# Loading W's second chunk in the last attention group, and a new order of the first two tiles' work

## The reference, cut to what matters

```
x = x + xattn(layernorm(x), ctx, ctx)          # x, ctx: (8, 512, 2048)
    per head and channel: corr = ifft(fft(q) * conj(fft(k))) over 512 positions
    w, idx = top_k(corr, 12);  w = softmax(w)
    out[p] = sum_i w_i * v[min(idx_i + p, 511)]
n = layernorm(x)
x = x + n @ W + bias + (n @ A_b) @ B_b + (n @ A_s) @ B_s   # W: 2048 x 2048
    A_b, B_b: rank 32, summed over 16 adapters by the batch's gate
```

## Time and profile before

| | |
|---|---|
| median of 3 runs | 3106.81 us (3106.17 to 3109.11) |
| the profiled execution's own time | 3107.9 us |
| its span, first to last instruction | 3106.1 us |
| PE busy | 3018.6 us, 97% |
| DVE, POOL, ACT busy | 2077.8, 1659.4, 1120.5 us |
| mean granted TensorE clock | 0.990 of full speed |

### The profile page before, as it was taken

One profiled execution on the slowest core, in us unless ns is written; L12 is line 12 of the kernel. 1 busy time (PEld: TensorE's weight loads), 2 busy tenths in 40 slices (PEclk: granted clock), 3 DMA queues, 4 the chain that ended last, 5 costly groups with the idle time before them and its releaser, 6 DMA issues. The chain is left out here.

```text
span 3106.1 us, 37964 instructions
## 1 busy us (share of the span) xinstructions
PE 3018.6 (97%) x14387; PEld 1647.6 (53%) x14387; DVE 2077.8 (67%) x2742; ACT 1120.5 (36%) x1696; POOL 1659.4 (53%) x753
## 2 busy tenths in 40 slices
PE   5999999999999999999977999999999999999999
PEld 3566565665656566665643444444444444444444
DVE  6889898989989999999994445444444443344322
ACT  4666666666656666555521011110111111011100
POOL 4898898988979898988842122221221122112210
PEclk9999999999999999999998999999999999999999
DMA  6334434344444534334159444345344534434321
GB/s 229 134 125 150 153 135 170 119 156 146 136 162 146 173 135 165 126 129 160 64 191 267 155 132 125 117 136 150 105 130 125 145 105 134 153 109 136 95 79 41
DMA packets 281220, 430.27 MB, mean 139 GB/s; under 512 B 147489, under 2 KB 164001, under 8 KB 265633
## 3 DMA queue, kind: packets, MB, share of 16 engines
q1 hardware_dynamic: 145888, 394.43, 36.7%
q10 hardware_dynamic: 135168, 33.57, 6.0%
HBM read 308.15 MB, written 86.25 MB: 127 GB/s over the span
## 5 line engine op out<-in xcount | busy, mean ns | idle before, releaser
L1439 PE MATMUL ps<-w_hi,h_hi 128*128 128x512 f16 x2048 | 776.5, 379 | 1.8 <-PEq L308 1.8
L1440 PE MATMUL ps<-w_lo,h_hi 128*128 128x512 f16 x2048 | 776.4, 379 | 0.0
L1441 PE MATMUL ps<-w_hi,h_lo 128*128 128x512 f16 x2048 | 776.4, 379 | 0.0
L1313 POOL TENSOR_TENSOR xt<-xt,vl 128x2048 f32<-128x2048 f32 x31 | 139.8, 4509 | 890.2 <-DMA xt<-x_scratch 653.9
L887 PE MATMUL ps<-op,it 128*128 128x512 f32 x1024 | 447.4, 595 | 12.8 <-DVE op L1034 12.8
L805 PE MATMUL ps<-wt,fp 128*128 128x512 f16 x1536 | 338.8, 380 | 2.1 <-DVE wt L1001 1.4
L1441 PEld LDWEIGHTS ps<-w_hi,h_lo 128*128 128x128 f16 x2048 | 200.5, 98 | 241.8 <-issue 0.3
L1439 PEld LDWEIGHTS ps<-w_hi,h_hi 128*128 128x128 f16 x2048 | 200.8, 98 | 238.9 <-issue 3.2
L887 PEld LDWEIGHTS ps<-op,it 128*128 128x128 f32 x1024 | 195.1, 191 | 247.4 <-issue 230.9
L1440 PEld LDWEIGHTS ps<-w_lo,h_hi 128*128 128x128 f16 x2048 | 200.5, 98 | 234.9 <-issue 0.6
L805 PEld LDWEIGHTS ps<-wt,fp 128*128 128x128 f16 x1536 | 150.5, 98 | 184.7 <-issue 2.2
(11 more groups left out here) (191 smaller groups left out, 5724.8 us busy)
## 6 DMA issues: line engine op xcount, KB each, us to landing
sg<-lora_ab SPq DMA_DIRECT2D x112, 512.0 KB, 4.8
xv<-x SPq DMA_DIRECT2D x33, 1024.0 KB, 5.2
cg<-ctx SPq DMA_DIRECT2D x32, 1024.0 KB, 5.2
x_scratch<-xv SPq DMA_DIRECT2D x32, 1024.0 KB, 4.2
xt<-x_scratch SPq DMA_DIRECT2D x32, 1024.0 KB, 5.1
out<-xt SPq DMA_DIRECT2D x31, 1024.0 KB, 4.0
xg<-x SPq DMA_DIRECT2D x30, 1024.0 KB, 8.0
xrow<-x SPq DMA_DIRECT2D x24, 1024.0 KB, 5.0
```

The lines of the kernel that those rows point to most:

```text
L1313: nc.gpsimd.tensor_tensor(xt[:, k, :], xt[:, k, :], vl[:, :], ALU.add).then_inc(vl_ok, 1)
L1439: nc.tensor.matmul(ps[:, c, :], h_hi[k][:, i, :], w_hi[c][:, i, :], start=(i == 0), stop=False)
L1440: nc.tensor.matmul(ps[:, c, :], h_hi[k][:, i, :], w_lo[c][:, i, :], start=False, stop=False)
L1441: last = nc.tensor.matmul(ps[:, c, :], h_lo[k][:, i, :], w_hi[c][:, i, :], start=False, stop=(i == KT - 1))
```

## The change

Memory: `early` grows by W's chunk 1 without the rest of its second half (`w_hi1`, `w_lo1`, 24 KB a partition); `spe` and `spo` become two tensors each, and `eo` moves, so that these 24 KB lie over tensors that the last group no longer uses. The rest stays as the kernel has it, with the indices adapted.

```diff
@@ attention, SP @@
+                    def second_chunk_of_w():
+                        sp.wait_ge(hi_sum, 2 * NG - 2)
+                        sp.wait_ge(w_ready, 4 * NG)
+                        for part in range(2):
+                            ks = slice(part * KT // 2, (part + 1) * KT // 2)
+                            sp.dma_start(early["w_hi1"][:, ks, :], w_pair[0, ks, :, 512:1024].rearrange("k p o -> p k o")).then_inc(s_w[2 + part], 16)
+                        sp.dma_start(early["w_lo1"][:, :, :], w_pair[1, 0:KT // 2, :, 512:1024].rearrange("k p o -> p k o")).then_inc(s_w[2], 16)
...
                             load_weights(b, g, 1)
                             if last and g == GPB - 2:
                                 first_rows_of_x2()
+                            if last and g == GPB - 1:
+                                second_chunk_of_w()
@@ attention, GpSimd, ahead of the loops @@
                     fold_q(0, 1)
+                    pool.wait_ge(cp_sum, 2)
                     rest_of_u(0, 1)
@@ attention, ACT @@
                     def step(b, g, more, lead, far, rows, convert, first=False):
                         transposed_out(b, g)
-                        if first:
-                            high_of_u(0, 2)
-                        if convert:
+                        if convert and not first:
                             weights_high(b, g, 0)
                         if more:
                             high_of_q(*ahead(b, g, 2))
-                        if rows:
+                        if rows and not first:
                             row_statistics(b, g)
                         if lead:
                             turn_row(*ahead(b, g, 1))
+                        if first:
+                            weights_high(b, g, 0)
+                            row_statistics(b, g)
...
-                        if convert:
+                        if convert and lead:
                             weights_high(b, g, 1)
...
                     divide_w(0, 0)
+                    high_of_u(0, 2)
                     normalise(0, 2)
                     act.wait_ge(eps_ok, 2)
-                    step(0, 0, True, True, True, True, False, True)
-                    for g in range(1, GPB):
+                    for g in range(GPB):
                         step(0, g, True, True, True, True, False)
...
-                        step(B // 2, g, True, True, True, True, True)
+                        step(B // 2, g, True, True, True, True, True, g == 0)
...
                         act.dma_start_transpose(early["h_lo0"][:, q * KT // 2:(q + 1) * KT // 2, :], h_rest[q]).then_inc(s_hl[q], 16)
+                    weights_high(B - 1, GPB - 1, 1)
@@ attention, DVE @@
                         if convert:
                             weights_rest(*convert, 1)
+                        if adapter:
+                            add_adapter(*adapter)
                         dve.wait_ge(z_ok, 4 * m + 4)
...
-                    def step(b, g, lead, convert, first=False):
+                    def step(b, g, lead, convert, first=False, last_sum=False):
                         w_rest(b, g)
-                        if first or not convert and later(b, g):
+                        if not convert and later(b, g):
                             add_adapter(*ahead(b, g, -1))
...
-                        if convert:
+                        if convert and not first:
                             weights_rest(b, g, 0)
                         if not lead:
                             statistics_of_x2()
+                            scale_of_x2()
                         products_even(b, g)
+                        if first:
+                            weights_rest(b, g, 0)
                         products_odd(b, g, lead)
                         if lead:
-                            top_lags(*ahead(b, g, 1), (b, g) if convert else None)
+                            top_lags(*ahead(b, g, 1), (b, g) if convert else None, (b, g) if last_sum else None)
                         elif convert:
+                            rest_of_x2()
                             weights_rest(b, g, 1)
-                            scale_of_x2()
-                            rest_of_x2()
                         add_output(b, g)
@@ multiplication, SP @@
+                    load_w_low(1, 1)
                     sp.wait_ge(s_ab0, 16)
...
-                    load_w(1, 0)
-                    load_w(1, 1)
                     sp.wait_ge(s_wst, 32 * 2 * KT)
@@ multiplication, ACT @@
+                    normalise(0, 1)
+                    act.wait_ge(s_st, 16 * NG)
+                    high_of_h(0, 1)
                     act.wait_ge(s_row, 48)
                     high_of_ab(0)
-                    act.wait_ge(s_st, 16 * NG)
-                    for t in range(TT):
+                    high_of_ax(0, 0)
+                    for t in range(1, TT):
                         step(0, t, True)
@@ multiplication, PE @@
-                            if c == 0 and i == KT // 2 and later(b, t):
+                            if c == (0 if later(b, t) else 3) and i == KT // 2:
                                 transpose_ax(b, t, gated)
...
                     chunk(0, 0, 0, False)
+                    chunk(0, 0, 1, False)
                     bounds(0, 5, 2 * P)
+                    chunk(0, 0, 2, False)
                     adapter_in(0, 0)
-                    transpose_ax(0, 0, False)
-                    for t in range(TT):
+                    chunk(0, 0, 3, False)
+                    adapter_out(0, 0, True)
+                    adapter_in(0, 1)
+                    for t in range(1, TT):
                         step(0, t, True, True)
@@ multiplication, DVE @@
-                        if c:
+                        if c == 3 or c and later(b, t):
                             dve.wait_ge(d_ok, 4 * n + c + 1)
...
                     nc.vector.memset(b_lo[2 * RANK:4 * RANK, :], 0.0).then_inc(b_zero, 1)
+                    statistics(0, 1)
+                    rest_of_h(0, 1)
                     dve.wait_ge(s_row, 48)
...
                     rest_of_ab(0)
+                    finish(0, 0, 0)
+                    finish(0, 0, 1)
+                    finish(0, 0, 2)
                     adapter(0, 0)
-                    for t in range(TT):
+                    gated_part(0, 0, 0)
+                    rest_of_ax(0, 0)
+                    gated_part(0, 0, 1)
+                    dve.wait_ge(y_ok, 3)
+                    add_adapter(0, 0)
+                    finish(0, 0, 3)
+                    adapter(0, 1)
+                    for t in range(1, TT):
                         step(0, t, True, True)
```

More of the change, by code:

```diff
@@ L621, in store_spectrum @@
                         act.wait_ge(spec, 4 * m + 1)
-                        nc.scalar.activation(spe[:, k, which, 0::2, :], ps[:, even, :].unsqueeze(1).broadcast_to([P, 2, GC]),
+                        nc.scalar.activation(spe[k][:, which, 0::2, :], ps[:, even, :].unsqueeze(1).broadcast_to([P, 2, GC]),
                                              ACT.Copy).then_inc(kept, 1)
                         act.wait_ge(spec, 4 * m + 2)
-                        nc.scalar.activation(spe[:, k, which, 1, :], ps[:, even + 1, :], ACT.Copy, scale=nyq[:, 0:1]).then_inc(kept, 1)
+                        nc.scalar.activation(spe[k][:, which, 1, :], ps[:, even + 1, :], ACT.Copy, scale=nyq[:, 0:1]).then_inc(kept, 1)
                         act.wait_ge(kept, 4 * m + 1)
-                        nc.scalar.activation(spe[0:1, k, which, 2, :], ps[0:1, even + 1, :], ACT.Copy).then_inc(kept, 1)
+                        nc.scalar.activation(spe[k][0:1, which, 2, :], ps[0:1, even + 1, :], ACT.Copy).then_inc(kept, 1)
                         if later(b, g) and later(b, g - 1):
@@ L630, in store_spectrum @@
                         act.wait_ge(spec, 4 * m + 4)
-                        nc.scalar.activation(spo[:, k, which, :, :], ps[:, odd:odd + 2, :], ACT.Copy, scale=(-1.0, 1.0)[which]).then_inc(kept, 1)
+                        nc.scalar.activation(spo[k][:, which, :, :], ps[:, odd:odd + 2, :], ACT.Copy, scale=(-1.0, 1.0)[which]).then_inc(kept, 1)
                     def corr_to_sbuf(b, g):
@@ L1034, in products_odd, with top_lags @@
                         nc.vector.tensor_tensor(op[:, 1, OI, :], ps[:, 7, :], cr[:, 1, :], ALU.subtract).then_inc(hi_sum, 1)
-                    def top_lags(b, g, convert):
+                    def top_lags(b, g, convert, adapter=None):
                         m = GPB * b + g
@@ L1143, in _ @@
                         step(0, g, True, False)
-                    with dve.Fori(1, B // 2) as b:
+                    with dve.Fori(1, B // 2 - 1) as b:
                         for g in range(GPB):
                             step(b, g, True, False)
+                    for g in range(GPB):
+                        step(B // 2 - 1, g, True, False, False, g == GPB - 1)
                     largest_of_rows()
@@ L1165, in build @@
```

(24 more changed lines are left out.)

44 lines of the change are left out of this document (23 added, 21 removed).

## The result

The changed kernel takes 3112.96 us in the median (3108.87 to 3115.80, 20 runs), the kernel before 3107.08 beside it (3104.89 to 3109.39, 20 runs). The ratio is 1.0015, with an interval of 1.0009 to 1.0021: slower by some 5 us, within the 0.2% that I had called no change, and within the range. The forecast was +2.4. The profiled execution took 3110.65 us with a span of 3108.9, against 3106.1 before: +2.8 there.

What follows compares the result with a forecast made beforehand. PE, busy 97% of the span, was taken to bound the kernel. The terms -2.3 - 0.7 + 0 + 5.4 = +2.4 gave 3110.3 us for the profiled execution and 3109.2 for the median, range 3100.5 to 3115.

Steps and rivals of the forecast that it cites:

- Part 1: First groups: GpSimd held for DVE's two sums and group 2's conversion moved ahead gain 2.3 us, between 1 and 5.
- 1.0 us is left of 3.8: First groups: the correlation starts 3.8 us sooner, but GpSimd's moved row subtraction slows DVE's folds, leaving 1.0.
- The upper end: First groups: without GpSimd's subtraction slowing the folds, the gain would be 3.8 + 1.3 = 5.1 us.
- Part 2: First converting group, near 887 us: the wait moves to before the lower spectra; 0.7 us gained, between 0 and 2.4.
- Part 3: End of attention: early loads of W and the moved last W piece change nothing at the hand-over, zero.
- Part 4: First tile of the multiplication: PE waits for DVE work queued behind gated sums; 5.4 us lost, between 1 and 8.5.
- the two waits that the forecast named: First tile: adapter_out waits for rest_of_ax behind three gated sums, adapter_in of tile 1 for add_adapter behind three more.
- PE idle after chunk 3 until a gated sum ends, twice: First tile: a sign that the forecast is right, with PE's clock at half in these waits.
- three more cost 2.2 to 4.4; I take the middle, 3.3: First tile: three more transposes among W's loads delay the first gated sum by 3.3 us.
- The slower rival: First tile: transposes hold W's queue 2.9 us each, first gated sum at 1706.2, +8.5 net, 3115.3 us; chance 20%.
- is first in the new burst: First tile: chunk 1's last MB of W lands near 1660, with 8 us to spare.
- The faster rival: First tile: the sums don't gate and PE alone sets tile 0, 9.0 us sooner, 3094.8 us; chance 10%.

Runs made afterwards that it cites:

- part 1 alone: The kernel before with only the first groups' two edits (GpSimd's wait for two sums, group 2's conversion ahead of normalisation): 3103.3 us, ratio 0.9985.
- parts 1 and 2: The kernel before with the first groups' edits and the first converting group's reordering, without early load, old multiplication: 3101.75 us, ratio 0.9982.
- Sums behind: The changed kernel with tile 0's six gated sums placed on DVE behind the work that PE waits for: 3108.74 us, ratio 1.0005.
- transposes held: As "Sums behind", but tile 1's four transposes wait until all of W is in: 3107.79 us, ratio 1.0001.
- old order: The changed kernel's attention and early load of W, with the multiplication in the order of the kernel before: 3104.68 us, ratio 0.9990.

## Why the prediction was right or wrong

**The result** lay in the range and on the forecast side, as a sum of two errors: the gain in attention was larger than I said, and so was the loss in the first tile. In the profile they are 4.6 and 5.0 us and cancel almost wholly, so that its 3110.65 us against the forecast 3110.3 are luck. The medians moved by 5.9 us, not 2.4.

**Part 1: 2.3 forecast, 4.9 in the profile of part 1 alone, 4.6 by its ratio.** The term that failed is "1.0 us is left of 3.8". I followed one chain, DVE's folds behind GpSimd, and its 1.5 us came out. I didn't look at the next thing for which DVE waited, the 2.26 us for ACT at 76.42: that wait hung on PE's correlation, which moved by 4. Contention took its toll, but not on a chain that set the end. The upper end, 3.8 + 1.3 = 5.1, was nearer. The Trainium skill's rule (SBUF — State Buffer, Who interferes with whom), that a VectorE instruction with two SBUF inputs and a GpSimd one that reads SBUF exclude each other, fits the two sums: 2.93 and 3.36 us beside GpSimd, 1.22 us each with it held. The folds didn't test it, for they ran when the subtraction had ended; what was held, var_eps, has one tensor input and isn't a case of the rule as I used it.

**Part 2: 0.7 forecast, nothing that can be measured.** Each step stood in the trace: the wait at 887 went, one of 3.8 came before the lower spectra behind the W piece on ACT. The profiles of parts 1 and 2 against part 1 alone show no gain in this group.

**Part 3: 0 forecast.** The block started 7.6 us sooner in the changed kernel's profile, but 4.4 to 7.7 us, 5.8 on the mean, in the seven other kernels with parts 1 to 3, against 5.9 for parts 1 and 2 and 4.9 for part 1 alone. So part 3 shows no gain, and parts 2 and 3 together are worth some 1 us. Much of the spread is there by group 1 already: its correlation starts 3.2 to 5.6 us sooner in the ten kernels, all with the same two edits of the first groups, and 5.3 sooner in the changed one. At the other end the last group's spectra took 12.26 us before and 12.51 in part 1 alone, 10.53 in eight of the nine kernels with part 2 and 11.97 in the ninth. Where they took longer the granted clock was still at its lower level beside them (0.50 from 1605 to 1610 us in part 1 alone, 0.99 in the changed kernel). Why, no run shows.

**Part 4: 5.4 forecast, 10.4 measured.** Of the two waits that the forecast named, one came: adapter_in waits 8.28 us for the additions, behind six sums, and the clock is at half behind that idle. The other didn't. I had PE at the end of chunk 3 near 1705, which is +52.2, and then waiting for DVE's axT behind three sums; it got there at +59.9, because W was late for chunk 3 too, and axT was ready. So my sign "PE idle after chunk 3 until a gated sum ends, twice" came once. "Sums behind" parts the two delays: with the sums gone adapter_in comes 7.1 us sooner and is still 1.4 late. The six sums took 13.3 us (13.8), the additions 2.73 (2.72), the slow stretch 2.4 (2.5). The term that failed is "three more cost 2.2 to 4.4; I take the middle, 3.3". Held back, four transposes free 8.7 us of the load queue, nearly the whole 9.0 us of the 3 MB. The slower rival had the size: 2.9 each, a first sum at 1706.2, which is +53.4, and +53.9 was measured. I had divided the ACT queue's share of the span by its transposes, a mean over all 128 of the program, and had read the landing of 9.4 us beside W's loads as waiting only. By the figure of the Trainium skill (DMA: Bandwidth & Descriptors, Latency and other measured facts), 261 GB/s, which the page gives for a middle dimension that isn't contiguous, three cost an estimated 3.0 us; the 2.2 us of each in this stretch don't bear that out.

**A cause I had not seen.** I wrote that W's last MB of chunk 1 "is first in the new burst" only to ask whether it is there in time. That it stands ahead of the adapter's tables, and that the maxima wait for these, costs 3 to 4 us in the old order (the wait 10.90 against 7.89 us, the rest 1456.4 against 1452.5). In the new one chunk 1 covers part of it: with the transposes held, PE's wait for the bounds is 0.67 us.

**The faster rival** (the sums don't gate) is refuted for the changed kernel, but half true once mended: with sums and transposes out of the way adapter_in of tile 1 comes at +56.3, 5.3 us sooner than before. Only 1.7 us of it are left at the end.

**What stays open:** by what rule a transpose costs the loads time. Four issued while some of W was still to be issued cost 8.7 us together; one issued behind all of W cost 3 us at +34.7 and some 2 at +37.7, and two at +38.3 and +41.5 nothing. The price falls as less of W is on its way, but no run holds all else equal, and a rule by order of issue alone doesn't fit: in "sums behind" a load with two of the four transposes ahead of it, issued 5.7 us ahead of the third, landed 7.4 us late.

## What to carry to other kernels

When a wait is removed, walk on to the next two waits of the same engines before costing what is left: part of them hang on the engine just freed. A reordering that fills PE's idle puts other work of VectorE, ACT and the load queue in front of PE: list, for each wait that the new order has, every instruction queued ahead of its releaser, loads included. Price a transposing DMA by what it does to the loads beside it, and hold it until most of a burst of loads has landed; that the last load has been issued was not enough here.

## What the hardware showed that I had not expected

- Four transposes of 256 KB among W's loads held these up by 8.7 us (last load at +52.0 against +43.4), with 201 to 217 GB/s in place of 350; two transposes issued at +38.3 and +41.5, when all of W was in the queue and its last load 5 us from landing, held it up by nothing and landed 8.5 and 6.1 us later. One issued at +34.7, also behind all of W, held it up by 3 us.
- A few plain loads do it the other way round as well: with two adapter loads released among them, a transpose took 11.3 us to land in place of 3.2.
- Filling the queues also stops the engine that issues: in the changed kernel ACT was held 8.61 us in the issue of one transpose (1.25 to 1.36 us in the run with the transposes held), and the next piece of its work, the scaled high part of A, had 10.03 us of idle in front of it.
- A VectorE instruction on 128x4 elements with one tensor input took 2.43 us beside GpSimd's subtraction, where it had taken 0.16, and the one ahead of it 1.09.
